# First expert group prepared inside the layers' last slots, and the softmax inverse placed behind a pass's third exponential

## The chip, the cores and the metric

One NeuronCore of one Trainium2 chip runs the whole program. The metric is the device time of one execution in microseconds (us), from the first to the last instruction and what lies around them. TensorE (PE), VectorE (DVE), ScalarE (ACT) and GpSimd (POOL) each run their own instruction list in order; SyncE (SP) issues all DMAs. They meet only at semaphores. An instruction that waits holds up everything behind it on its engine.

## The reference, cut to what matters

The input x is 32 sequences of 256 rows of 128 floats. Computed is `x1 = x + layers(layernorm(x))` and `out = x1 + experts(layernorm(x1))`.

```
h = layernorm(x)
for l in range(4):
    xn = ln(h) * w + b
    q, k, v = xn@Wq.T+bq, xn@Wk.T+bk, xn@Wv.T+bv            # 16 heads of width 8
    scores = (q.k + rel_shift((q+u).r)) * 8**-0.5, causal mask
    h = h + (softmax(scores) @ v) @ Wo.T + bo
    h = h + gelu(ln(h) @ W1.T + b1) @ W2.T + b2              # 512 wide
# experts: 16 of width 32 plus a shared one of width 256
s = sigmoid(xn @ router.T); sb = s + bias
keep the best 2 of 4 groups of experts, then the best 4 experts
w = s[chosen] / sum;  out = shared(xn) + sum_e w_e * down_e(silu(gate_e xn) * up_e xn)
```

## The kernel before, in words

**Layers.** `layers_program` treats (layer, sequence) as one index n from 0 to N-1 = 127 and is a software pipeline written out by hand: slot s of `SLOTS = range(-1, N + 6)` holds f1/f2/values of sequence s, the maxima scores of s-2, the attention scores of s-3 and s-4, the product with v of s-4, the output projection of s-5 and the feed-forward part of s-6. Each engine's block walks the same slots, with its own order inside a slot. Slots 0 to 127 are the body, 128 to 133 the tail in which ever fewer stages are live.

**The softmax division.** A column of ones in `v_pad` makes the product with v also give the denominators. ACT copies both out (`context_copy`, L850), SP sends the denominators to `ctx_den` and the numerators to `ctx_num` (L489, L492), ACT turns `ctx_den` into its inverse by a Ln and an Exp with scale -1 (`inverse`, L855 and L857), POOL multiplies (`normalize_context`, L1207), and PE's projection `b3` (L697) reads the product. `inverse(s - 5)` stands on ACT ahead of the three exponentials of rounds 1, 4 and 2 of sequence s-4 (`exp_round`, L818), and behind the copies `xn1T_out` (L826) and `xn2T_out` (L832). `split_first` (L841), gelu between two loads of activation tables (L902, L904), `context_copy` and the exponentials 5, 0, 3 follow.

**POOL's slot.** v_padded, xn2_split, normalize_context(s-5), turned(s-1) (L1185 to L1191), the next sequence's power (`power_in` for the first layer, L1131 to L1136; `power` for the others, L1140 and L1142), add_row twice (L1219), power of the second norm, xn1_split (L1167, L1169). In every 32nd slot `split_qkv` (L1150, L1152) stands at the slot's end.

**SP's slot.** The turned rows of q (L473, waits for `turned`), the maxima's rows (L481), the exchange (L453), the context (L489, L492), the q and k rows (L463, L465), and a load of weights or of x here and there. PE's `a_scores` round 5 (L656) waits for the maxima's rows to land.

**PE's slot.** Attention scores of rounds 1, 4, 2 among maxima scores, f2, values, up, `b3`, two products with v, maxima round 3, attention rounds 5, 0, 3, down (half), transposes, down (half).

**Experts.** `experts_program` runs after a barrier in a second block with 16 groups of 512 rows, again as slots, q from -1. In slot -1 group 0 is transposed, rounded in two parts (`exT_parts`), routed on DVE by a chain of small operations that wait for one another (L1589 to L1641), and the expert weights are split (L1557, L1559); POOL normalizes group 1 (`norm`, L1714). Already before the barrier, in slots N+3 and N+4 on DVE and N+4, N+5 on POOL, the residual and statistics of groups 0 and 1 and the norm of group 0 are made (L1033 to L1061, L1250, L1253).

The code of the four functions' places is printed here.

Of the kernel before, what the change touches and what calls it, by code (L numbers as in the profile page):

```python
# [28 lines left out]

# [16 lines left out]
N = LAYERS * B  # L46
# [37 lines left out]
EXP_SET, GELU_SET = "natural_log_exp_and_others", "gelu_and_others"  # L84
# [85 lines left out]
class Early:  # L170
# [17 lines left out]
    xn_ready: object  # L188


def early_parts(nc, ctx):
# [4 lines left out]
    def sem(name):  # L196
        return ctx.enter_context(nc.semaphore(name))

    return Early(
# [6 lines left out]
        ve_ready=sem("eve_ready"), rstd_ready=sem("erstd_ready"), xn_ready=sem("exn_ready"))  # L206


def layers_program(nc, a, h_all, ex):

    with ExitStack() as ctx:
# [9 lines left out]
        w_qkv = sb("w_qkv", [128, LAYERS, 3 * D])  # L221

# [34 lines left out]
        qstack = sb("qstack", [128, RING, PLACES, S], F32R)  # L257
        kstack = sb("kstack", [128, RING, PLACES, S], F32R)
# [262 lines left out]
        def _(pe):  # L521
# [213 lines left out]

            pe.wait_ge(first_landed, 32)

            for s in SLOTS:
# [37 lines left out]
                if live(s - 5):  # L776
                    b3(s - 5)
                if live(s - 4):
                    pv(s - 4, 1)
# [30 lines left out]
                if live(s - 6):  # L810
                    down(s - 6, 1)

        @block.scalar
        def _(act):
# [64 lines left out]
            for s in SLOTS:  # L879
# [4 lines left out]
                if live(s - 5):  # L884
                    inverse(s - 5)
# [4 lines left out]
                if live(s - 4):  # L890
                    exp_round(s - 4, 2)
                if s == 0:
# [22 lines left out]
        def _(dve):  # L915
# [154 lines left out]

            stats_1(0)
            for s in SLOTS:
# [48 lines left out]
                if s == N + 3:  # L1121
                    experts_stats()
                if s == N + 4:
                    experts_norm()
                    experts_stats_second()

        @block.gpsimd
        def _(pool):
# [109 lines left out]
            for s in SLOTS:  # L1238
# [4 lines left out]
                if live(s - 5):  # L1243
                    normalize_context(s - 5)
                if live(s - 1):
                    turned(s - 1)
                if s in (N + 4, N + 5):
                    g = s - N - 3
# [23 lines left out]
                if live(s + 4) and (s + 4) % B == 0 and s > 0:  # L1272
                    split_qkv(layer(s + 4))


def experts_program(nc, a, h_all, out, ex):
# [7 lines left out]
    with ExitStack() as ctx:  # L1284
# [14 lines left out]
        w_in_parts = sb("w_in_parts", [128, 2, 2 * GU], F32R)  # L1299
# [3 lines left out]
        xT = sb("exT", [128, 2, GT, 128])  # L1303
        xT_parts = sb("exT_parts", [128, 2, 2, GT, 128], F32R)
        score = sb("score", [128, GT, E])
        biased = sb("biased", [128, GT, E])
        larger = sb("larger", [128, GT * G, 2])
        smaller = sb("smaller", [128, GT * G, 2])
        tops = sb("tops", [128, 3, GT * G])
        gs = sb("gs", [128, GT, 14])  # L1310
        gtop = sb("gtop", [128, GT, 8])
# [474 lines left out]
```

## Time and profile before

| what | value |
|---|---|
| runs | 2225.02, 2231.17, 2236.08 us (median 2231.17) |
| profiled execution | 2229.07 us, span 2227.3 us |
| PE busy | 2152.8 us (97%) |
| PE weight loads busy | 1876.5 us (84%) |
| DVE, ACT, POOL busy | 1906.0 (86%), 1796.5 (81%), 1288.4 us (58%) |
| mean granted clock of PE | 0.988 |

The span is what lies between the first and the last instruction; the execution's own time is 1.77 us more. The barrier between the two blocks lies near 1956 us of the span. Busy means that the engine executed something other than waiting. Records of one engine may overlap by about 0.1 us.

### The profile page before, as it was taken

Reading aid. Unit: us, or ns where it says so; the run is one execution under the profiler, and the core shown is the slowest. Engines: PE = TensorE matmul, PEld = TensorE weight load, DVE = VectorE, ACT = ScalarE, POOL = GpSimd, SP = SyncE. Lnnn points to the kernel's source line nnn. Section 1 sums busy time; section 2 is a strip of 40 time slices with the busy share of each in tenths; the row PEclk is TensorE's granted clock in tenths of the full one; section 3 lists DMA queues with packets and bytes.
Section 4 is the critical chain, followed back from the end, with each engine's and each line's share of the span. In section 5 each row is a group of like instructions: output and inputs, shape, how many; then the busy total and the mean of one; then the engine's idle time right before and its main releaser. Section 6 shows DMA issues by size and latency. Waiting matters only on the chain. (4 is left out here: it accounts for less than half of the span.)

```text
span 2227.3 us, 80806 instructions
## 1 busy us (share of the span) xinstructions
PE 2152.8 (97%) x30224; PEld 1876.5 (84%) x30224; DVE 1906.0 (86%) x4659; ACT 1796.5 (81%) x2661; POOL 1288.4 (58%) x2277
## 2 busy tenths in 40 slices
PE   4899999999999999999999999999999999879999
PEld 3788888888888888888888888888888888768888
DVE  6789888888888888888888888888888888479996
ACT  2688888888888888888888888888888888845543
POOL 4555665566555555566555655565555555456774
PEclk8899999999999999999999999999999999979999
DMA  4444444444434444344443443344334444124443
GB/s 120 124 122 129 126 131 128 111 115 114 110 109 112 116 112 117 108 113 115 111 111 110 114 121 109 106 113 116 110 109 120 120 116 111 40 61 110 97 115 83
DMA packets 279984, 246.79 MB, mean 111 GB/s; under 512 B 38960, under 2 KB 270256, under 8 KB 279600
## 3 DMA queue, kind: packets, MB, share of 16 engines
q1 hardware_dynamic: 279600, 241.63, 40.0%
q8 instruction: 246, 4.03, 0.8%
q14 instruction: 138, 1.13, 0.2%
HBM read 31.24 MB, written 4.72 MB: 16 GB/s over the span
## 5 line engine op out<-in xcount | busy, mean ns | idle before, releaser
L1003 DVE TENSOR_REDUCE rowmax<-bank 128x4 f32<-128x1024 f32 (+1 forms) x768 | 916.3, 1218 | 149.5 <-PE bank L597 149.0
L818 ACT ACTIVATE probs<-bank 128x1024 f32<-128x1024 f32 x768 | 737.6, 1024 | 94.2 <-PE bank L656 82.9
L656 PE MATMUL bank<-qstack,kstack 64*128 64x128 f32 (+1 forms) x4096 | 423.2, 299 | 7.5 <-DMA qstack<-maxrows 7.3
L597 PE MATMUL bank<-kstack,qstack 62*128 62x256 f32 (+1 forms) x4096 | 417.7, 301 | 4.4 <-DMA qstack<-base_turned 4.4
L656 PEld LDWEIGHTS bank<-qstack,kstack 64*128 64x128 f32 x4096 | 315.0, 191 | 10.7 <-DMA qstack<-maxrows 10.1
L597 PEld LDWEIGHTS bank<-kstack,qstack 62*128 62x128 f32 x4096 | 317.3, 193 | 4.6 <-issue 4.6
L1167 POOL CAST xn1T_parts<-xn1T 128x256 fp32r<-128x256 f32 x128 | 50.7, 396 | 425.0 <-ACT xn1T L826 425.0
L731 PE MATMUL bank<-w,hidden 128*128 128x128 f32 x2048 | 284.1, 282 | 3.5 <-ACT hidden L866 2.8
L619 PE MATMUL bank<-maskT_half,pick_half 64*128 64x128 bf16 (+1 forms) x3072 | 268.7, 240 | 15.9 <-ACT probs L818 6.0
L676 PE MATMUL bank<-probs,v_pad 128*32 128x256 f32 x4096 | 271.0, 382 | 0.6 <-DVE v_tok L984 0.6
L559 PE MATMUL bank<-mask_half,pick_half 64*128 64x128 bf16 (+1 forms) x3072 | 269.5, 243 | 1.7 <-ACT xn1T L826 0.7
L731 PEld LDWEIGHTS bank<-w,hidden 128*128 128x128 f32 x2048 | 249.6, 192 | 21.7 <-issue 4.1
L1140 POOL TENSOR_SCALAR ve<-mv 128x2 f32<-128x2 f32 x224 | 49.6, 221 | 312.9 <-DVE mv L940 304.8
L841 ACT ACTIVATE base<-bank,b_cols 128x256 fp32r<-128x256 f32 x256 | 107.5, 470 | 130.6 <-PE bank L131 130.6
L866 ACT ACTIVATE hidden<-bank,b 128x256 f32<-128x256 f32 x512 | 200.6, 475 | 4.8 <-PE bank L131 3.3
L619 PEld LDWEIGHTS bank<-maskT_half,pick_half 64*128 64x128 bf16 x3072 | 116.6, 94 | 67.9 <-DVE rowmax L1003 24.9
L1142 POOL TENSOR_TENSOR rstd<-ve,expo 128x2 f32<-128x2 f32 x224 | 161.1, 719 | 18.7
L676 PEld LDWEIGHTS bank<-probs,v_pad 128*32 128x32 f32 x4096 | 117.3, 109 | 60.1 <-issue 0.8
L902 ACT ACT_TABLE_LOAD x128 | 164.2, 1283 | 2.3
L904 ACT ACT_TABLE_LOAD x128 | 164.2, 1283 | 2.3
L683 PEld LDWEIGHTS bank<-probs,v_pad 128*32 128x32 f32 x4096 | 122.4, 110 | 44.0
L683 PE MATMUL bank<-probs,v_pad 128*32 128x128 f32 x4096 | 158.7, 273 | 0.0
(147 smaller groups left out, 5008.9 us busy)
## 6 DMA issues: line engine op xcount, KB each, us to landing
qstack<-base SPq DMA_DIRECT2D x384, 128.0 KB, 2.6
kstack<-base SPq DMA_DIRECT2D x384, 128.0 KB, 2.6
qstack<-base_turned SPq DMA_DIRECT2D x384, 128.0 KB, 2.5
turn_x<-turn_c SPq DMA_DIRECT2D x512, 32.0 KB, 1.8
ctx_den<-ctxT_raw SPq DMA_DIRECT2D x256, 64.0 KB, 2.0
ctx_num<-ctxT_raw SPq DMA_DIRECT2D x256, 64.0 KB, 2.0
factors<-rows_kept SPq DMA_DIRECT2D x64, 256.0 KB, 4.8
h_all<-in_x SPq DMA_DIRECT2D x16, 256.0 KB, 3.2
```

The source lines that it names most:

```text
L559: pe.matmul(v[:, :, c:c + 64], pick_half[rows, half], mask_half[rows, half, 0:heads], start=(half == 0), stop=True, skip_group_check=True)
L597: last = pe.matmul(bank[:, b0 + b, i * wide:(i + 1) * wide], qstack[rows, r, p0 + i, t * 128:(t + 1) * 128], kstack[rows, r, p0 + i, 0:wid ...
L619: pe.matmul(v[:, :, c:c + 64], pick_half[rows, 2 + half], maskT_half[rows, half, 0:heads], start=(half == 0), stop=True, skip_group_check= ...
L656: last = pe.matmul(bank[:, b0 + b, i * wide:(i + 1) * wide], kstack[rows, r, p0 + i, kt * 128:(kt + 1) * 128], qstack[rows, r, p0 + i, q0: ...
L676: pe.matmul(bank[32 * c:32 * c + 32, PV_BANK, c0:c0 + S], v_pad[:, v, 0, 4 * half + c, w], x, start=(j == 0), stop=True, skip_group_check= ...
L683: last = pe.matmul(bank[32 * c:32 * c + 32, PV_BANK, c0 + 128:c0 + S], v_pad[:, v, 1, 4 * half + c, w], x, start=False, stop=True, skip_gr ...
L731: last = pe.matmul(bank[:, DOWN_BANK, t * 128:(t + 1) * 128], hidden[:, c, t * 128:(t + 1) * 128], w_2[:, layer(n), c], start=(c == 0), st ...
L818: act.activation(probs[:, k], bank[:, A_BANK[k]:A_BANK[k] + 2, :], ACT.Exp, scale=SCALE).then_inc(exp_done[k], 1)
L866: act.activation(hidden[:, c], bank[:, UP_BANK[c // 2], (c % 2) * S:(c % 2 + 1) * S], ACT.Gelu, bias=b_1[:, layer(n), c:c + 1]).then_inc(g ...
L902: act.preload_act_table_set(GELU_SET)
L904: act.preload_act_table_set(EXP_SET)
L1003: dve.tensor_reduce(rowmax[:, n % 2, t, :, p0:p0 + heads], bank[:, M_BANK[k]:M_BANK[k] + 2, :].rearrange("p b (h c) -> p b h c", h=heads), ...
```

## The change

There are two parts. In the first, the tiles and semaphores that group 0 of the experts needs move to the `Early` record that both programs share. `w_in_parts` now lies in the space of `qstack`, `exT_parts` in `kstack`, `exT` and the routing tiles in `w_qkv`, which are free late in the layers; so the new steps wait until their last readers are done. The routing functions become the class `Routing`, with the same operations. The statistics of group 0 and group 1 come two slots earlier; the experts' weights are split in slot N+2; group 0 is transposed in N+3 and routed in N+4. The experts' program then skips group 0's preparation and group 1's norm, which POOL does at the end of slot N+4.

In the second, `inverse` moves behind `exp_round(s - 4, 2)` on ACT, and `normalize_context` moves behind `turned` and the two power steps on POOL.

```
 PE, layers_program
+    def experts_turn():
+        pe.wait_ge(ex.landed, 16 * EX_DMAS); pe.wait_ge(ex.xn_ready, 1); pe.wait_ge(exp_done[0], N)
+        for t in range(GT):
+            last = pe.transpose(bank[:, X_TURN_BANK, t*128:(t+1)*128], ex.xn[:, t], ex.eye[:])
+    def experts_router():
+        pe.wait_ge(ex.xT_ready, 1)
+        for t in range(GT): last = pe.matmul(bank[:, X_TURN_BANK, t*E:(t+1)*E], xT[:, 0, t], ex.w_router[:], ...)
...
         b3(s - 5)
+        if s == N + 4: experts_router()
...
         down(s - 6, 1)
+        if s == N + 3: experts_turn()
 ACT
-                if live(s - 5):
-                    inverse(s - 5)
                 exp_round(s - 4, 1); exp_round(s - 4, 4); exp_round(s - 4, 2)
+                if live(s - 5):
+                    inverse(s - 5)
...
                     gelu(s - 6)
-                    act.preload_act_table_set(EXP_SET)
+                    if s < N + 4:
+                        act.preload_act_table_set(EXP_SET)
+                if s == N + 4:
+                    act.preload_act_table_set(SIGMOID_SET)
+                    act.wait_ge(ex.logits_done, 1)
+                    act.activation(ex.score..., bank[:, X_TURN_BANK, 0:GT * E], ACT.Sigmoid).then_inc(ex.score_ready, 1)
 DVE
+            def experts_weights():
+                dve.wait_ge(scoresT_done[A_LAST], N - RING + 2)
+                dve.tensor_copy(w_in_parts[:, 0], ex.w_in[:]); dve.tensor_tensor(w_in_parts[:, 1], ..., ALU.subtract)
+            def experts_turned():
+                dve.wait_ge(ex.xn_turned, 1)
+                dve.tensor_copy(xT[:, 0], bank[:, X_TURN_BANK, :]); dve.tensor_copy(xT_parts[:, 0, 0], xT[:, 0])
+                dve.tensor_tensor(xT_parts[:, 0, 1], xT[:, 0], xT_parts[:, 0, 0].bitcast(F32), ALU.subtract)
...
-                if s == N + 3:
+                if s == N + 1:
+                    dve.wait_ge(scoresT_done[A_LAST], N - RING + 2); dve.wait_ge(v_done, N)
+                    dve.wait_ge(weights_now, LAYERS)
+                    routing.fill()
                     experts_stats()
-                if s == N + 4:
+                if s == N + 2:
                     experts_norm()
                     experts_stats_second()
+                    experts_weights()
+                if s == N + 3:
+                    experts_turned()
+                if s == N + 4:
+                    routing.routing_groups_1(0); routing.routing_groups_2(0)
+                    routing.routing_experts(0); routing.weights_of_experts(0)
 POOL
-                if live(s - 5):
-                    normalize_context(s - 5)
                 if live(s - 1):
                     turned(s - 1)
-                if s in (N + 4, N + 5):
+                if s in (N + 2, N + 3):
                     ... (wait for mv_ready, ve, power: as before)
                 (power_in(s + 1) or power(..., s + 1))
+                if live(s - 5):
+                    normalize_context(s - 5)
                 add_row(s - 6, b_2, ...)
...
+                if s == N + 4:
+                    pool.wait_ge(ex.rstd_ready, 2); pool.wait_ge(ex.xn_turned, 1)
+                    for t in range(GT): last = pool.tensor_scalar(ex.xn[:, t], h_all[:, 2 + t // 2, t % 2], ...)
+                    last.then_inc(ex.xn_ready, 1)
 experts_program: every `if live(q + 1)` step of x_turn, router, xT_out, scores, low and routing gets
+ and q + 1 > 0
 norm(q + 2) is skipped for q + 2 = 1; the memsets of the routing tiles and the weights' split are gone;
-                load_table(2 * q, ACT.Sigmoid)
+                load_table(2 * q - 1, ACT.Sigmoid)
...
+            act.wait_ge(ex.route_filled, 2)
+            load_table(0, ACT.Silu)
```

## Rows read from the trace of the kernel before

**Rows 1.** Waits over the whole span: total us, times, longest us.

```profile
PEld bank L656 <- DMA qstack<-maxrows: 10.1, 14, 2.3
PEld bank L619 <- ACT probs L818: 9.1, 18, 1.4
```

**Rows 2.** Timeline of ACT, one first-layer slot: start, us, line; idle before, releaser.

```profile
263.81 2.86 ACT L818 ACTIVATE probs<-bank 128x1024 f32<-128x1024 f32 x3 [0.49 <-PE bank L656]
...
267.43 0.44 ACT L855 ACTIVATE ctx_den<-ctx_den 128x256 f32<-128x256 f32 x1
...
272.27 0.84 ACT L841 ACTIVATE base<-bank,b_cols 128x256 fp32r<-128x256 f32 x2 [0.89 <-PE bank L131]
```

**Rows 3.** The same timeline of ACT, the next slot's first exponentials.

```profile
278.43 2.86 ACT L818 ACTIVATE probs<-bank 128x1024 f32<-128x1024 f32 x3 [0.49 <-PE bank L656]
```

**Rows 4.** Timeline of POOL in the same first-layer slot.

```profile
269.98 0.73 POOL L1207 TENSOR_TENSOR ctx_num<-ctx_num,ctx_den 128x256 f32<-128x256 f32 x1
270.67 0.73 POOL L1185 TENSOR_TENSOR turn_x<-turn_s,turn_x 128x256 f32<-128x256 f32 x1
...
273.30 1.04 POOL L1136 TENSOR_TENSOR rstd<-ve,expo 128x4 f32<-128x4 f32 x1
```

**Rows 5.** Timeline of PE's weight loads, the projection of that slot.

```profile
273.83 0.53 PEld L697 LDWEIGHTS bank<-w_o,ctx_num 128*128 128x128 f32 x4
```

**Rows 6.** Timeline of POOL in a slot of the third layer.

```profile
1025.25 0.72 POOL L1142 TENSOR_TENSOR rstd<-ve,expo 128x2 f32<-128x2 f32 x1
```

**Rows 7.** Timeline of PE's weight loads, the projection of that slot.

```profile
1025.99 0.53 PEld L697 LDWEIGHTS bank<-w_o,ctx_num 128*128 128x128 f32 x4
```

**Rows 8.** Timeline of POOL, the slot after a split of the next layer's weights.

```profile
1372.12 0.40 POOL L1150 CAST w_now<-w_qkv 128x256 fp32r<-128x256 f32 x1
...
1378.01 0.72 POOL L1142 TENSOR_TENSOR rstd<-ve,expo 128x2 f32<-128x2 f32 x1
```

**Rows 9.** Timeline of PE's weight loads: that slot's projection.

```profile
1377.59 0.53 PEld L697 LDWEIGHTS bank<-w_o,ctx_num 128*128 128x128 f32 x4
```

**Rows 10.** Timeline of PE's weight loads: the wait for the maxima behind it.

```profile
1382.95 0.19 PEld L656 LDWEIGHTS bank<-qstack,kstack 64*128 64x128 f32 x2 [1.46 <-DMA qstack<-maxrows]
```

**Rows 11.** Timeline of ACT, a slot in which the denominators landed late.

```profile
1417.92 0.42 ACT L855 ACTIVATE ctx_den<-ctx_den 128x256 f32<-128x256 f32 x1 [1.22 <-DMA ctx_den<-ctxT_raw]
```

**Rows 12.** Timeline of PE's weight loads in the same slot.

```profile
1419.75 0.10 PEld L619 LDWEIGHTS bank<-maskT_half,pick_half 64*128 64x128 bf16 x2 [1.08 <-ACT probs L818]
```

**Rows 13.** Timeline of DVE in the tail and across the barrier.

```profile
1928.33 0.42 DVE L1069 TENSOR_TENSOR h_all<-bank,h_all 128x256 f32<-128x256 f32 x1 [3.90 <-PE bank L731]
...
1947.02 1.38 DVE L1061 TENSOR_SCALAR exn<-h_all,emv,erstd 128x128 f32<-128x128 f32 x4
...
1949.93 0.38 DVE L1055 BATCH_NORM_AGGREGATE emv<-estats 128x2 f32<-128x6 f32 x4
...
1957.52 1.76 DVE L1559 TENSOR_TENSOR w_in_parts<-w_in,w_in_parts 128x1536 fp32r<-128x1536 f32 x1
```

**Rows 14.** Timeline of PE's weight loads, the projection of sequence 126.

```profile
1932.49 0.53 PEld L697 LDWEIGHTS bank<-w_o,ctx_num 128*128 128x128 f32 x4
```

**Rows 15.** Timeline of POOL in the tail and across the barrier.

```profile
1943.83 0.71 POOL L1142 TENSOR_TENSOR rstd<-ve,expo 128x2 f32<-128x2 f32 x1
1946.34 0.40 POOL L1176 CAST xn2T_parts<-xn2T 128x256 fp32r<-128x256 f32 x1 [1.80 <-ACT xn2T L832]
...
1958.63 1.76 POOL L1701 TENSOR_TENSOR exT_parts<-exT,exT_parts 128x512 fp32r<-128x512 f32 x1 [6.18 <-ACT exT_parts L1511]
1960.39 3.17 POOL L1714 TENSOR_SCALAR exn<-h_all,emv,erstd 128x128 f32<-128x128 f32 x4
1966.08 1.28 POOL L1701 TENSOR_TENSOR exT_parts<-exT,exT_parts 128x512 fp32r<-128x512 f32 x1 [2.53 <-ACT exT_parts L1511]
```

**Rows 16.** Timeline of PE behind the barrier.

```profile
1956.53 0.63 PE L1423 MATMUL ebank<-eeye,exn 128*128 128x128 f32 x4 [1.18 <-PEq L211]
...
1963.61 1.12 PE L1423 MATMUL ebank<-eeye,exn 128*128 128x128 f32 x4 [4.11 <-POOL exn L1714]
```

More of the change, by code:

```diff
@@ L28 @@
 from dataclasses import dataclass
+import math
 import numpy as np
@@ L197, in sem, with part @@
         return ctx.enter_context(nc.semaphore(name))
+    qstack, kstack = (sb(name, [128, RING, PLACES, S], F32R) for name in ("qstack", "kstack"))
+    w_qkv = sb("w_qkv", [128, LAYERS, 3 * D])
+    w_flat, used = w_qkv[:].rearrange("p l c -> p (l c)"), [2 * GT * 128]
+    def part(*shape):
+        lo, n = used[0], math.prod(shape)
+        used[0] += n
+        flat = (w_flat[:, lo:lo + n] if used[0] <= LAYERS * 3 * D else sb(f"route_part{lo}", [128, n])[:])
+        return flat.rearrange("p (a b) -> p a b", a=shape[0]) if len(shape) == 2 else flat
     return Early(
@@ L734, in down @@
                     last.then_inc(down_done, 1)
+            def experts_turn():
+                pe.wait_ge(ex.landed, 16 * EX_DMAS)
+                pe.wait_ge(ex.xn_ready, 1)
+                pe.wait_ge(exp_done[0], N)
+                for t in range(GT):
+                    last = pe.transpose(bank[:, X_TURN_BANK, t * 128:(t + 1) * 128], ex.xn[:, t], ex.eye[:])
+                last.then_inc(ex.xn_turned, 1)
+            def experts_router():
+                xT = ex.xT()
+                pe.wait_ge(ex.xT_ready, 1)
+                for t in range(GT):
+                    last = pe.matmul(bank[:, X_TURN_BANK, t * E:(t + 1) * E], xT[:, 0, t], ex.w_router[:],
+                                     start=True, stop=True)
+                last.then_inc(ex.logits_done, 1)
             pe.wait_ge(first_landed, 32)
@@ L1471, in _ @@
             for q in SLOTS:
-                if live(q + 1):
+                if live(q + 1) and q + 1 > 0:
                     x_turn(q + 1)
@@ L1479, in _ @@
                     down(q - 1, 0)
-                if live(q + 1):
+                if live(q + 1) and q + 1 > 0:
                     router(q + 1)
@@ L1540, in _ @@
                     rows_out(q)
-                if live(q + 1):
+                if live(q + 1) and q + 1 > 0:
                     scores(q + 1)
@@ L1635, in weights_of_experts @@
[L1635 to L1642 removed]
+            routing = Routing(dve, ex, apart_dve)
@@ L1668, in _ @@
                     gating(q, 0)
-                if live(q + 1):
-                    routing_groups_1(q + 1)
+                if live(q + 1) and q + 1 > 0:
+                    routing.routing_groups_1(q + 1)
                 if live(q - 1):
@@ L1676, in _ @@
                     gating(q, 2)
-                if live(q + 1):
-                    routing_groups_2(q + 1)
+                if live(q + 1) and q + 1 > 0:
+                    routing.routing_groups_2(q + 1)
                 if live(q - 1):
@@ L1682, in _ @@
                     gating(q, 3)
-                if live(q + 1):
-                    routing_experts(q + 1)
+                if live(q + 1) and q + 1 > 0:
+                    routing.routing_experts(q + 1)
                 if live(q - 1):
@@ L1688, in _ @@
                     gating(q, 4)
-                if live(q + 1):
-                    weights_of_experts(q + 1)
+                if live(q + 1) and q + 1 > 0:
+                    routing.weights_of_experts(q + 1)
                 if live(q):
@@ L1724, in _ @@
             for q in SLOTS:
-                if live(q + 1):
+                if live(q + 1) and q + 1 > 0:
                     low(q + 1)
@@ L1728, in _ @@
                     power(q + 2)
-                if live(q + 2) and q + 2 > 0:
+                if live(q + 2) and q + 2 > 1:
                     norm(q + 2)
```

289 lines of the change are left out of this document (176 added, 113 removed).

## The prediction, on record before the changed kernel ran

> **What bounds the kernel now.** I read the page's busy shares first (PE 97%), then the waits over the whole span, then the timelines of ACT, POOL and PE's weight loads for a few slots side by side. The body of the layers repeats every 14.62 us: the exponentials of rounds 5, 0, 3 start at 263.81 and again at 278.43 [rows 2, 3], and most body slots have that length. In such a slot PE is never idle for more than a few tenths; it sets the length. The reader is to see two disturbances on top. When the maxima's rows land late, PE waits for them before attention round 5: 10.1 us in 14 waits [rows 1]. When the denominators land late, the inverse waits on ACT, the exponential of round 1 stands behind it, and PE waits for that exponential: 9.1 us in 18 waits [rows 1]; in one slot the inverse waited 1.22 us and PE 1.08 us [rows 11, 12].
>
> **The inverse behind the third exponential, ACT.** Nothing is added: Ln and Exp are 0.44 us each [rows 2]. Between the third exponential and `split_first` ACT idles 0.89 us for PE [rows 2], so the pair lands in that gap and `split_first` stays where it is, with no more than about 0.1 us at risk. If the gap is gone (a late pass), `split_first` and with it the cosines are late by what is missing. What it takes away: PE's waits for the first exponential. Of the 9.1 us I take away 7, since a part lies in the tail, where the exponentials themselves are late; bounds 0 and 9.
>
> **The product with the inverse, POOL.** This is where the change costs. POOL's list is dense from the split of xn1 to the second `add_row`, so moving the 0.73 us product behind `turned` and the power pulls these 0.69 us forward (270.67 - 269.98 [rows 4]) and ends the product where the power ended, plus 0.04. Nothing waits on the moved ones: their inputs, the exchange and the statistics, are microseconds old.
>
> - First layer. The power (four columns) ended at 273.30 + 1.04 = 274.34 [rows 4], so the product ends at 274.34 - 0.69 + 0.73 = 274.38. PE's projection began loading it at 273.83 [rows 5]. PE waits 0.55 us, with the handover 0.57. Behind that instruction on PE stand both products with v, maxima round 3, attention rounds 5, 0, 3; ACT's exponentials and so the next xn1 and POOL's next list hang on these, so the wait comes back every slot and nothing gives it back. 26 slots (projection live and next sequence still in layer 0) x 0.57 = +14.8 us. Bounds: 0 (PE has slack that records with modelled ends hide) and 26 x 0.65 = 17.
> - Other layers. The power ended at 1025.97 [rows 6]; the product ends at 1026.01, against a load at 1025.99 [rows 7]: 0.02, with the handover 0.04. 95 slots x 0.04 = +3.8 us. This is a tie within the resolution of the records; bounds -0.1 (no wait, 0 us) and 0.2 per slot (19 us). I take the value of the rows.
> - The slot after a split of the next layer's weights. There POOL starts 1.15 us late (1372.12 on [rows 8]). The old product was early enough to hide that; the new one ends at 1378.73 + 0.04 = 1378.77 against a load at 1377.59 [rows 9]: 1.18 us. Three such slots: +3.5 us; bounds 0 and 4.
> - The turned rows of q are ready 0.69 us earlier. SP's list waits for them, and the maxima's DMAs stand behind them, so these go out up to 0.69 us earlier as well; in the first layer PE comes 0.57 us later on top. That covers most of the 14 waits, and the one of 1.46 us behind the late POOL slot [rows 10], where PE itself now comes 1.2 us later. I take away 7 of the 10.1 us; bounds 0 and 10.
>
> Body: 14.8 + 3.8 + 3.5 - 7 - 7 = +8.1 us.
>
> **The tail.** In slots 127 to 130 the exponentials end close to the projection, so the inverse behind them makes the projection late by some tenths each; I take +1.0 in all (bounds 0 and four times 0.57, 2.3). In slot 131 POOL now makes group 1's power ahead of the product for sequence 126. It waits for group 1's statistics, and these start on DVE only after the residual add that ends at 1928.75 [rows 13]: norm of group 0 and the statistics last 1949.93 + 0.38 - 1947.02 = 3.3 us [rows 13], so they end at 1932.05. The add of 0.22 and the four-column power of 1.04 [rows 4] with their handovers give 1933.5, the product 1934.2, against a load at 1932.49 [rows 14]: +1.8 us, and the product with v, the last context and all that follows hang on it. In slot 132 the norm of group 1 (3.17 us [rows 15]) stands on POOL from the end of the power at 1944.54; the split of the last xn2 was at 1946.34 [rows 15] and can start at 1947.71: +1.4 us on the chain that ends the layers. The other additions are hidden: the filling and statistics of slot 129 in DVE's idle time before the next projection, group 0's transposes and router product in PE's idle time (they cost under 1.5 us), the split of xT where the statistics stood, the sigmoid's table load behind the gelu while ACT waits for the last xn2, and the routing chain between the last two residual adds. If that cover is gone, the routing would cost up to 7 us. Tail: +4.2 us; bounds 1 and 9.
>
> DVE's split of the expert weights (its second operation 1.76 us [rows 13]) now falls beside POOL's power and product. The rows show what such a meeting costs POOL: the rounding remainder took 1.76 us beside that operation and 1.28 alone [rows 15], so about 0.5. The Trainium skill's page SBUF — State Buffer (two separate sides) says the port pair that the two share is held for a whole instruction and the loser is blocked until its end. By the row the meeting costs 0.5, by the rule up to 1.76 us; the sum leaves it out as the overlap may not happen, and the range holds both.
>
> **The experts' start.** PE's first work is now the transposes of group 1, which it did at 1963.61 after POOL's norm, 4.11 us idle ahead of it; it can do them where group 0's stood, at 1956.53 [rows 16]: -7.1 us. Everything behind is as before. The x of group 2 is still only requested at the barrier, and the first gating stands behind its residual: +0.5 (bounds 0 and 2). That the transposes took 0.63 us at first and 1.12 us later [rows 16] tells that PE is slow in this stretch; how long it stays so may move by some us either way, which I put at nothing. Start: -6.6; bounds -8 and -2.
>
> **Sum.** 8.1 + 4.2 - 6.6 = +5.7 us on the profiled execution's own 2229.07: 2234.8 us. The runs' median is 2.1 us above that execution, so an offset of this size stays inside the band.
>
> **Rivals.**
> - The projection has slack. For it: the load at 273.83 need not be what PE needed at that moment, since loads run ahead of the matmuls. Against it: PE's list is in order and the load is followed within a tenth by its matmul. Then the body is 3.5 - 14 = -10.5, the whole -12.9: 2216 us.
> - Slower: the tie in layers 2 to 4 goes the wrong way. Place: POOL's list before the projection; price: 95 slots times what the chain is longer than the rows say, through the new neighbours of `turned` and power on DVE or a context that lands later. At 0.2 us per slot it is 19 instead of 3.8: +20.9, 2250 us. It decides from 0.11 per slot on (2241.5).
> - The late landings cost the same elsewhere. The transfers are as late as before, and PE waits for them at the projection or at round 5. For it: the SP list is itself full in slots with a load. Against: the inverse now has 3 us more. Both sevens return: +14, 2249 us.
> - Part one does nothing: the first products wait for something else (the factors' transfer, PE at low clock), and only the tail's costs stay: +6.6, 2241 us.
>
> **Chances and range.** Forecast 0.56; projection with slack 0.14; the tie lost 0.16; landings unchanged 0.08; part one without effect 0.06. About 0.5% (11 us) can be told from no change: below 2220 faster, above 2242 slower. So faster 0.14, same 0.62, slower 0.24. Range 2221 to 2249: it leaves out the first rival and the far end of the second. The forecast's own range is 2227 to 2241.
>
> **What would show it.** Right: POOL's product starts behind the power in every body slot; PE's projection load has an idle time of about 0.6 us with POOL as releaser in the first layer, next to none or under 0.1 in the others, about 1.2 in three slots; body slots of 15.2 and 14.65 us; the waits for probs and maxima down to a few us; the layers ending near 1956 + 12 us; group 1's transposes less than 1 us behind the barrier. Wrong: first-layer slots of 14.6 us, or later ones of 14.8 and more, or experts that last as long from the barrier as before.

## The result and the profile after

The changed kernel takes 2237.97 us (median of 14 runs, 2233.64 to 2241.83), the kernel before 2227.9 us on the same chips (14 runs). The ratio is 1.0042 [1.0031, 1.0054]: slower by 0.4%, inside what the forecast called the same, 3 us above its number. The change itself was larger than forecast: 10 us between the medians and 6.3 us between the two profiled executions, against a forecast of 5.7. The profiled execution has a span of 2233.6 us against 2227.3. Two terms of the sum were off by some 4 us each, in opposite directions. One run in what follows, of E6 with 2511.85 us, was in a slower state than all others and is left out of its ratio.

Where the 6.3 us between the two profiled executions lie is best seen by cutting both at the same instructions: the start of PE's first weight load for the output projection of a sequence, for PE's first work of the experts (before: group 0's transposes, after: group 1's, since group 0's are already done in the layers), and the end of the span. These are single executions, and runs of one kernel differ by some 5 us either way (2223.9 to 2236.1 for the kernel before), so a difference of 1 us in such a stretch is read only where rows show its cause.

| stretch, us | before | after | difference |
|---|---|---|---|
| start to the 2nd projection | 96.1 | 97.1 | +0.9 |
| layer 0 (25 slots) | 371.8 | 381.2 | +9.4 |
| layers 1 to 3 (96 slots) | 1412.9 | 1411.8 | -1.1 |
| last 5 projections | 60.6 | 68.3 | +7.7 |
| last projection to the experts' first PE work | 15.1 | 15.2 | +0.1 |
| from there to the end | 270.8 | 260.1 | -10.7 |

The waits over the whole span (engine, waiting tile and line, what it waited for: us in total, times, longest). L851 is the projection, L773 the first product with v, which reads the exponentials:

```profile
PEld bank L851 <- POOL ctx_num L1419: 26.3, 33, 3.9
PEld bank L773 <- ACT probs L992: 1.8, 2, 0.9
```

From the page's groups of instructions (busy, mean ns of one, idle time before them), attention's loads with the maxima:

```profile
L810 PEld LDWEIGHTS bank<-qstack,kstack 64*128 64x128 f32 x4096 | 315.6, 191 | 0.5 <-DMA qstack<-maxrows 0.4
```

So both kinds of late landing are nearly gone: 10.1 us for the maxima became 0.4, and 9.1 us for the exponentials 1.8 [rows 1]. A new wait of 26.3 us stands at the projection. One slot of layer 0 shows it; the timelines of ACT, POOL and PE's loads (start, duration, instruction, idle time before it and its releaser) answer to [rows 2 to 5]:

```profile
277.01 0.42 ACT L1031 ACTIVATE ctx_den<-ctx_den 128x256 f32<-128x256 f32 x1
277.55 0.84 ACT L1015 ACTIVATE base<-bank,b_cols 128x256 fp32r<-128x256 f32 x2
```
```profile
275.29 0.73 POOL L1397 TENSOR_TENSOR turn_x<-turn_s,turn_x 128x256 f32<-128x256 f32 x1
277.95 1.04 POOL L1348 TENSOR_TENSOR rstd<-ve,expo 128x4 f32<-128x4 f32 x1
278.96 0.73 POOL L1419 TENSOR_TENSOR ctx_num<-ctx_num,ctx_den 128x256 f32<-128x256 f32 x1
```
```profile
279.73 0.52 PEld L851 LDWEIGHTS bank<-w_o,ctx_num 128*128 128x128 f32 x4 [0.55 <-POOL ctx_num L1419]
```

The reader is to see that the inverse's second half (L1031) ends at 277.43, 1.5 us before the product (L1419) starts: ACT does not hold the product, POOL's own list does. The product ends at 279.69, and PE, idle 0.55 us, loads 0.04 us later. In a slot of the third layer the product directly follows a two-column power of 0.73 and there is no such wait; in the slot behind a split of the next layer's weights there is one of 1.12 us:

```profile
1021.24 0.73 POOL L1354 TENSOR_TENSOR rstd<-ve,expo 128x2 f32<-128x2 f32 x1
1021.94 0.73 POOL L1419 TENSOR_TENSOR ctx_num<-ctx_num,ctx_den 128x256 f32<-128x256 f32 x1
...
1389.93 0.72 POOL L1419 TENSOR_TENSOR ctx_num<-ctx_num,ctx_den 128x256 f32<-128x256 f32 x1
```
```profile
1390.71 0.52 PEld L851 LDWEIGHTS bank<-w_o,ctx_num 128*128 128x128 f32 x4 [1.12 <-POOL ctx_num L1419]
```

The slots last 15.22 us in layer 0 and 14.67 in the others, against 14.60 to 14.62 for an undisturbed slot before.

The tail is where more was lost than forecast. POOL, DVE and PE in slot 131 (answering to [rows 13, 14]):

```profile
1942.63 0.85 POOL L1460 TENSOR_SCALAR eve<-emv 128x4 f32<-128x4 f32 x1 [2.86 <-DVE emv L1235]
1943.56 2.51 POOL L1463 TENSOR_TENSOR erstd<-eve,expo 128x4 f32<-128x4 f32 x1
1946.05 0.72 POOL L1419 TENSOR_TENSOR ctx_num<-ctx_num,ctx_den 128x256 f32<-128x256 f32 x1
```
```profile
1942.46 0.93 DVE L1254 CAST qstack<-w_in 128x1536 fp32r<-128x1536 f32 x1
1943.42 1.76 DVE L1256 TENSOR_TENSOR qstack<-w_in,qstack 128x1536 fp32r<-128x1536 f32 x1
```
```profile
1946.82 1.22 PE L851 MATMUL bank<-w_o,ctx_num 128*128 128x128 f32 x4 [3.68 <-POOL ctx_num L1419]
```

One slot earlier, without DVE beside it, the same two instructions took 0.23 and 1.04 us:

```profile
1928.88 0.23 POOL L1460 TENSOR_SCALAR eve<-emv 128x4 f32<-128x4 f32 x1 [1.96 <-DVE emv L1220]
1929.20 1.04 POOL L1463 TENSOR_TENSOR erstd<-eve,expo 128x4 f32<-128x4 f32 x1
```

The first ends at 1943.48, 0.09 us behind the cast's end (1943.39), and the second at 1946.07, 0.9 behind the subtraction's end (1945.18). Alone they need 0.23 and 1.04 us, so each ended as if it had done all but 0.15 us of its work after DVE's instruction: 0.62 and 1.47 us were lost. The Trainium skill's page SBUF — State Buffer (SBUF: two separate sides) says that the port pair is held for a whole instruction and the loser blocked until its end. This trace agrees.

The 0.5 us that I took from [rows 15] was the price of a short meeting only. POOL's operation there started at 1958.63, when 0.65 us of DVE's subtraction was left (it ended at 1957.52 + 1.76 [rows 13]); it could lose no more than that, and lost 0.48.

The experts' start, PE behind the last residual add (DVE L1249, at 1972.62 + 0.42):

```profile
1973.53 0.63 PE L1618 MATMUL ebank<-eeye,exn 128*128 128x128 f32 x4 [1.01 <-PEq L367]
```

Group 1's transposes stand 0.49 us behind the end of the layers, where they stood 7.7 us behind it [rows 16]. Beyond these 7.2 us another 3.6 were gained. The windows (start:end and length, busy time of PE, PE's loads, DVE, ACT, POOL with their counts, granted clock as a share, DMA share, GB/s) of the first 40 us of experts, before and then after:

```profile
1956.50:1976.50 20.00, 14.43 (x48) 11.40 (x49) 15.21 (x75) 10.88 (x19) 10.61 (x12) 0.57 0.40 95
1976.50:1996.50 20.00, 17.01 (x81) 14.33 (x80) 15.24 (x68) 8.47 (x15) 11.95 (x13) 0.83 0.33 74
```
```profile
1973.50:1993.50 20.00, 14.89 (x70) 11.64 (x71) 15.20 (x66) 12.43 (x22) 11.89 (x12) 0.91 0.41 103
1993.50:2013.50 20.00, 20.00 (x112) 17.75 (x112) 14.86 (x69) 8.47 (x16) 12.01 (x13) 0.84 0.29 68
```

Before, the granted clock of the first 20 us was 0.57, near the lower of its two levels (1.2 GHz of 2.4 GHz, a share of 0.5); after, it was 0.91.

### The profile page after: what moved, and what is told of

It reads as the page before. It is cut to its first block and busy times, and to the rows that moved or that the text cites. A ratio compares the mean times of both kernels' runs of the same rounds, so it can differ in the third digit from the quotient of the medians.

```text
span 2233.6 us, 80802 instructions
## 1 busy us (share of the span) xinstructions
PE 2157.8 (97%) x30224; PEld 1880.1 (84%) x30224; DVE 1908.5 (85%) x4662; ACT 1790.9 (80%) x2656; POOL 1289.3 (58%) x2276
## 5 line engine op out<-in xcount | busy, mean ns | idle before, releaser
L773 PE MATMUL bank<-maskT_half,pick_half 64*128 64x128 bf16 (+1 forms) x3072 | 267.0, 240 | 9.8 <-DVE turn_c L1150 2.4
L773 PEld LDWEIGHTS bank<-maskT_half,pick_half 64*128 64x128 bf16 x3072 | 117.2, 94 | 62.0 <-DVE rowmax L1183 27.0
L133 PE MATMUL bank<-xn2T_parts,w_parts 128*128 128x256 f32 x512 | 156.0, 305 | 2.2 <-POOL xn2T_parts L1390 1.6
```

Of the source, the lines that this page charges most:

```text
L133: pe.matmul(out, w[0], x[0], start=True, stop=False)
L773: pe.matmul(v[:, :, c:c + 64], pick_half[rows, 2 + half], maskT_half[rows, half, 0:heads], start=(half == 0), stop=True, skip_group_check= ...
```

## The experiments

The change has two halves: the experts' first group inside the layers (first part), and the inverse behind the third exponential with its product on POOL behind the power (second part). Times in the table are medians; the ratio is against the kernel before on the same chip, with its 95% interval. It is formed from all runs of both kernels, so it need not be the quotient of the medians. E1 to E4 ran on one chip, E5 to E8 on a second, E9 and E10 on a third, where the kernel before took 2225.0, 2227.8 and 2226.4 us, so kernels are compared by their ratios.

| kernel | us | ratio |
|---|---|---|
| after | 2238.0 | 1.0042 [1.0031, 1.0054] |
| E1 first part only | 2225.1 | 0.9985 [0.9968, 1.0002] |
| E2 second part only | 2242.8 | 1.0073 [1.0051, 1.0094] |
| E3 product behind `turned` | 2212.9 | 0.9942 [0.9922, 0.9962] |
| E4 experts' power behind the product | 2230.5 | 1.0025 [1.0012, 1.0038] |
| E5 E3, norm of group 1 later | 2213.0 | 0.9934 [0.9919, 0.9949] |
| E6 E5, DVE's weight split one slot earlier | 2214.2 | 0.9944 [0.9923, 0.9966] |
| E7 E3, inverse back in its old place | 2216.5 | 0.9950 [0.9933, 0.9967] |
| E8 inverse moved, product not | 2557.4 | 1.1477 [1.1432, 1.1522] |
| E9 second part only, product behind `turned` | 2216.6 | 0.9942 [0.9919, 0.9965] |
| E10 only the product behind `turned` | 2220.0 | 0.9964 [0.9947, 0.9982] |

And the stretches of their profiled executions, cut as above (the last column runs from the experts' first PE work to the end of the span):

| us | start | layer 0 | layers 1-3 | last 5 | to experts | experts |
|---|---|---|---|---|---|---|
| before | 96.1 | 371.8 | 1412.9 | 60.6 | 15.1 | 270.8 |
| after | 97.1 | 381.2 | 1411.8 | 68.3 | 15.2 | 260.1 |
| E1 | 97.2 | 371.1 | 1417.4 | 63.8 | 17.0 | 259.0 |
| E2 | 98.8 | 381.1 | 1411.1 | 64.4 | 15.6 | 272.6 |
| E3 | 97.5 | 369.3 | 1405.8 | 63.7 | 15.2 | 260.8 |
| E4 | 96.7 | 382.1 | 1412.2 | 63.7 | 15.2 | 259.2 |
| E5 | 97.9 | 369.0 | 1406.8 | 63.7 | 13.6 | 260.9 |
| E6 | 96.5 | 368.0 | 1407.5 | 63.6 | 13.6 | 260.6 |
| E7 | 96.5 | 369.8 | 1412.1 | 62.1 | 16.9 | 262.2 |
| E8 | 94.8 | 438.8 | 1686.7 | 70.1 | 15.2 | 260.5 |
| E9 | 97.1 | 367.6 | 1404.9 | 62.5 | 12.7 | 267.1 |
| E10 | 95.9 | 370.9 | 1407.6 | 60.3 | 13.9 | 270.3 |

**E1, the first part alone.**

```diff
+                if live(s - 5):
+                    inverse(s - 5)
                 if live(s - 4):
                     exp_round(s - 4, 1)
...
-                if live(s - 5):
-                    inverse(s - 5)
...
+                if live(s - 5):
+                    normalize_context(s - 5)
                 if live(s - 1):
                     turned(s - 1)
...
-                if live(s - 5):
-                    normalize_context(s - 5)
```

> Only the first part (group 0 of the experts prepared in the layers' last slots); inverse and product stand where they stood before. Theory (the body's loss comes from the product's new place on POOL, the experts' start gains about 11 us by the traces): body slots as in the kernel before (14.60 us and the old disturbances), tail longer by 1.4 us (norm of group 1 ahead of the last xn2 split) and 1.5 us (DVE's weight split ahead of a residual add), experts 10.9 shorter: about 8 us faster than before. Rival (the tail's additions cost what the start gains): within 3 us of before. Rival (the losses of the body come from the memory moves of the first part): slower than before by 5 us or more.

It measured 0.9985, -3 us, not to be told from nothing: the expected 8 us missed, and the rival in which the tail takes what the start gives came closest (within 3 us). The late landings are back, as large as before:

```profile
PEld bank L773 <- ACT probs L992: 12.0, 23, 1.4
PEld bank L810 <- DMA qstack<-maxrows: 11.1, 12, 2.4
```

The experts gained as in the changed kernel (270.8 to 259.0), but 5 us went in ahead of them: 3.2 in the last five projections and 1.9 behind these, and layers 1 to 3 took 4.5 more with their late landings. In this execution the first part alone moves a good part of its gain from the end of the kernel into the tail.

**E2, the second part alone**: the kernel before with the same two moves, in the other direction of E1's diff.

> Only the second part (inverse behind the third exponential, product behind the power). Theory: PE waits 0.54 us at the projection in each of 25 first-layer slots, 1.1 to 1.7 in three slots, 0.07 per slot in the others; maxima and exponential waits gone; body +9, tail +1.5, so about 10.5 us slower than before. If the parts added, first part -8 and second +10.5 would give +2.5 for both; both together showed +6 in the trace, and theory says that the difference is POOL's long power behind DVE in the tail, which only the pair has. Rival (the second part is neutral and the loss is an effect of both): within 3 us of before.

It measured 1.0073, some 16 us slower where 10.5 were expected. Its layers are those of the changed kernel to within 1 us in both stretches (its start is 1.7 us longer), and its waits are nearly the same:

```profile
PEld bank L697 <- POOL ctx_num L1207: 24.8, 33, 3.3
PEld bank L619 <- ACT probs L818: 1.8, 2, 0.9
PEld bank L656 <- DMA qstack<-maxrows: 1.4, 2, 1.2
```

So the new wait and the end of the two old ones belong to the second part alone. The experts, whose code is that of before, took 272.6 against 270.8 us, with a granted clock in their first two windows of 20 us of 0.66 and 0.74 against 0.57 and 0.83.

The halves add up within their intervals: 0.9985 x 1.0073 = 1.0058, against 1.0042 together.

**E3, the product one place earlier.** If the wait at the projection is POOL's order and not ACT's inverse, the product directly behind `turned` (ahead of the power) keeps what the second part gains and loses its price.

```diff
                 if live(s - 1):
                     turned(s - 1)
+                if live(s - 5):
+                    normalize_context(s - 5)
...
-                if live(s - 5):
-                    normalize_context(s - 5)
                 if live(s - 6):
                     add_row(s - 6, b_2, ...)
```

> Both parts, but POOL's product stands right behind the turned rows, ahead of every power step. Theory: the product then ends at about 1.0 us ahead of the projection in all slots but the three behind a weight split, so the 0.54 us waits (25 slots), the 0.07 (95 slots) and most of the three long ones go, while the turned rows keep their 0.69 us and the maxima do not return; the 3.9 us wait in the tail goes too: 14 + 6.5 + 2.5 + 3.5 less, 26 us faster than the changed kernel, 2211 to 2213 us, 0.7% faster than before. Rival (the late landings only hide behind the wait at the projection and come back when it goes): no more than 14 us faster than the changed kernel, 2224 us. Rival (the power behind the product becomes the late one: first norm's rstd on DVE): slots of 14.9 us or more in the first layer.

It measured 2212.9 us, 0.6% faster than the kernel before. By the ratios that is 22 us faster than the changed kernel (the 25 us between the medians come from two chips), where 26 were expected and the rival gave no more than 14. The wait at the projection fell from 26.3 to 3.9 us:

```profile
PEld bank L810 <- DMA qstack<-maxrows: 5.0, 8, 1.6
PEld bank L851 <- POOL ctx_num L1419: 3.9, 5, 1.6
...
POOL ctx_num L1419 <- ACT ctx_den L1031: 39.8, 123, 3.4
```

The last line is a wait that appears on POOL: 0.3 us per slot for the inverse. It costs next to nothing: the median slot is 14.63 us in layer 0 and 14.62 in the others, as an undisturbed one before. An engine's wait is a price only if its consumer is late, as the changed kernel shows from the other side: there POOL waits 5.0 us in all for the inverse, and the kernel is slower.

**E4, the experts' power behind the product**, in slots 130 and 131, all else as in the changed kernel. It takes two things off the product's path at once: the power itself, and the power's meeting with DVE on the port pair.

```diff
-                if s in (N + 2, N + 3):
-                    ... # wait for the statistics, add, power of group s - N - 1
                 if live(s + 1) and 0 < s + 1 < B:
                     power_in(s + 1)
...
                 if live(s - 5):
                     normalize_context(s - 5)
+                if s in (N + 2, N + 3):
+                    ...
```

> Both parts; on POOL only the experts' power steps of the two tail slots stand behind the product in place of ahead of it; the body is unchanged. Theory: the body stays at 15.22 and 14.67 us, the waits at the projections of sequences 125 and 126 fall from 0.7 and 3.9 us to 0.7 and about 0.6, about 3.5 us faster than the changed kernel. The four-column power itself still takes about 2.5 us beside DVE's weight split, off the path. Rival (the chain through the inverse on ACT is as long): under 1 us.

The last five projections went from 68.3 to 63.7 us, and the ratio from 1.0042 to 1.0025: 4 us, as expected (3.5), though the two intervals overlap. POOL (first fence) and DVE (second):

```profile
1943.85 1.08 POOL L1419 TENSOR_TENSOR ctx_num<-ctx_num,ctx_den 128x256 f32<-128x256 f32 x1 [3.12 <-ACT ctx_den L1031]
1944.91 1.74 POOL L1466 TENSOR_SCALAR eve<-emv 128x4 f32<-128x4 f32 x1
1946.72 1.04 POOL L1469 TENSOR_TENSOR erstd<-eve,expo 128x4 f32<-128x4 f32 x1
```
```profile
1943.42 0.93 DVE L1254 CAST qstack<-w_in 128x1536 fp32r<-128x1536 f32 x1
1944.39 2.16 DVE L1256 TENSOR_TENSOR qstack<-w_in,qstack 128x1536 fp32r<-128x1536 f32 x1
```

The power is back at 1.04 us, where the expectation kept it at 2.5. The meeting has not gone but moved: now the product met DVE's cast and took 1.08 us instead of 0.73, DVE's subtraction started beside the product and took 2.16 instead of 1.76, and the small operation ahead of the power took 1.74 instead of 0.23, off the product's path. E4 does not tell the price of the power's place from that of the meeting.

**E5, E3 with the norm of group 1 one slot later**, behind the split of the last xn2 and `add_row`, so that the split no longer stands behind 3.1 us of norm. **E6** moves DVE's split of the expert weights (`experts_weights`) from slot N+2 to N+1 on top.

```diff
+                if s == N + 5:
+                    ... # norm of group 1
...
-                if s == N + 4:
-                    ...
```

And E6 on top of it, on DVE:

```diff
                 if s == N + 1:
                     ...
+                    experts_weights()
                 if s == N + 2:
                     ...
-                    experts_weights()
```

> The kernel with the product right behind the turned rows, and POOL's norm of group 1 one slot later, behind the last xn2 split and row add. Theory: in the changed kernel the norm (3.14 us) ends and the last split starts at once, 0.9 us after its input; with the norm behind it the last split waits only for ACT's xn2T, so the layers end 0.9 to 1.4 us earlier and the experts start as before (the norm ends about 3 us ahead of the barrier): 1 us faster than the kernel with the product behind the turned rows, 2212 us. Rival (the norm then ends behind the barrier): no gain or a loss of up to 2 us in the experts' stage.

> As the kernel with the norm behind the split, and DVE's weight split in slot N+1 in place of N+2. Theory (DVE and POOL meet: DVE's split ahead of the residual add of sequence 126 delays it, and POOL's power beside it takes 2.5 us instead of 1.04): in N+1 DVE has 3.0 us idle ahead of the next residual add, so the split is hidden there, the four-column power of N+2 moves back to 1.04 us if no other DVE operation with two inputs from memory runs beside it, and that of N+1 becomes the long one; another 1 us faster. Rival (POOL's product for sequence 125 meets the split and is late by up to 2 us): no gain or 1 us slower.

E5's stretch from the last projection to the experts fell from 15.2 to 13.6 us. Of these 1.6 us, 1.3 lie where the norm stood: PE loads the last split xn2 6.23 us behind the last projection, against 7.52 in E3 and 6.24 in the kernel before. In the total that is too little to tell E5 (0.9934) from E3 (0.9942), though E5 has the lowest ratio of the study.

E6 brought nothing, and its rival says why: the product for sequence 125 now met DVE's subtraction, and PE waited 1.78 us for it where it had waited 0.72 in E5. POOL, DVE and PE's loads:

```profile
1912.14 1.78 POOL L1419 TENSOR_TENSOR ctx_num<-ctx_num,ctx_den 128x256 f32<-128x256 f32 x1 [3.31 <-ACT ctx_den L1031]
```
```profile
1911.58 1.76 DVE L1256 TENSOR_TENSOR qstack<-w_in,qstack 128x1536 fp32r<-128x1536 f32 x1
```
```profile
1913.97 0.52 PEld L851 LDWEIGHTS bank<-w_o,ctx_num 128*128 128x128 f32 x4 [1.78 <-POOL ctx_num L1419]
```

The later intervals were shorter in turn, and the last five projections took 63.6 us against 63.7.

**E7, E3 with the inverse back ahead of the exponentials.**

> As the kernel with the product behind the turned rows, but the inverse on ACT back ahead of the three exponentials. It separates what the move on ACT brings from what the move on POOL brings. Theory: the waits of PE for the exponential (5.9 us in the body's trace before, 8.8 in that with the first part alone) come back, the maxima's stay at a few us, since they hang on POOL's turned rows: body 5 to 8 us longer than with the product behind the turned rows, 2219 us. Rival (late transfers are one cause, and the exponential's waits were bought by the maxima's): the body differs by under 2 us. Rival (ACT's move brings nothing since the exponentials wait for PE anyway): under 1 us.

It measured 2216.5 us, 2 us more than E3 by the ratios (0.9950 against 0.9942), with intervals that overlap. In its profiled execution, which is 5 us above its median, layers 1 to 3 took 6.3 us more than in E3. The landings are late again for the exponentials:

```profile
PEld bank L773 <- ACT probs L992: 10.2, 19, 1.1
PEld bank L810 <- DMA qstack<-maxrows: 4.2, 3, 2.2
```

**E8, the inverse moved and the product not**: what the second part would be without its POOL half.

```diff
+                if live(s - 5):
+                    normalize_context(s - 5)
                 if live(s - 1):
                     turned(s - 1)
...
-                if live(s - 5):
-                    normalize_context(s - 5)
```

> Both parts, inverse behind the third exponential, but POOL's product where it stood before, ahead of the turned rows. Theory: POOL then waits for the inverse about 2.2 us in every slot, the turned rows, SP's issue and the maxima's rows land 2.2 us later, and PE waits at attention round 5 for about 2 us in nearly all slots: body slots of 16 to 17 us, 2227 + 120 * 1.7 = about 2430 us. Rival (the turned rows have room): under 2260 us.

It measured 2557 us in two runs, 14.8% slower, and worse than either theory (2430 us, and under 2260). POOL now waits for the inverse in every slot, `turned` stands behind it, and PE stands behind the maxima of the turned rows:

```profile
POOL ctx_num L1419 <- ACT ctx_den L1031: 288.4, 127, 3.4
...
PEld bank L810 <- DMA qstack<-maxrows: 247.7, 124, 3.4
```

That is 2 us per slot. The profile pages of the changed kernel (first) and of E8 show a second cost:

```profile
PE 2157.8 (97%) x30224; PEld 1880.1 (84%) x30224; DVE 1908.5 (85%) x4662; ACT 1790.9 (80%) x2656; POOL 1289.3 (58%) x2276
```
```profile
PE 2284.6 (89%) x30224; PEld 1992.5 (78%) x30224; DVE 2001.5 (78%) x4662; ACT 1806.3 (70%) x2656; POOL 1292.3 (50%) x2276
```

The span grew by 332.5 us (2566.1 against 2233.6). Of these PE was idle for 206 more and busy for 127 more, with the same number of matmuls, and its granted clock was 0.940 over the span against 0.989. So a slot takes 17.6 us on average and not the 16 to 17 of the theory, which had counted the waits alone. PE's timeline in a slot shows the same group of four matmuls at 0.48 us ahead of the wait and 0.78 behind it, and eight matmuls of the MLP at 1.77 and then 1.06:

```profile
1011.50 0.48 PE L751 MATMUL bank<-kstack,qstack 62*128 62x256 f32 x4
...
1013.99 0.33 PE L810 MATMUL bank<-qstack,kstack 64*128 64x128 f32 x2 [1.88 <-DMA qstack<-maxrows]
...
1014.88 0.78 PE L751 MATMUL bank<-kstack,qstack 62*128 62x256 f32 x4
...
1016.78 1.77 PE L885 MATMUL bank<-w,hidden 128*128 128x128 f32 x8
...
1019.04 1.06 PE L885 MATMUL bank<-w,hidden 128*128 128x128 f32 x8
```

**E9 and E10**, on the kernel before, without the first part: E9 moves the inverse and puts the product behind `turned`; E10 does only the latter.

```diff
-                if live(s - 5):
-                    normalize_context(s - 5)
                 if live(s - 1):
                     turned(s - 1)
+                if live(s - 5):
+                    normalize_context(s - 5)
```

> The kernel before with the inverse behind the third exponential and the product right behind the turned rows; nothing of the first part. Theory: body as with both parts and the product behind the turned rows, 10 us shorter than before by traces (disturbances gone), tail longer by 1 us, experts' stage unchanged: 9 us faster than before, ratio 0.996. With the second part as it was changed (1.0073) this says that one place on POOL is worth 25 us. Rival (the gain of 12 to 14 us with both parts came mostly from the experts' start): under 4 us faster.

> The kernel before with only POOL's product behind the turned rows; the inverse stays ahead of the exponentials. Theory: the maxima's waits of PE (7.8 us in the body) fall to 2 to 4, those for the exponential (5.9 us) stay: 4 to 5 us faster than before, ratio 0.998, and about 5 us slower than with the inverse moved as well. Rival (the order of transfers shifts late ones from one wait to the other): within 1 us of before.

E9 has the ratio of E3, 0.9942, with the experts left as they were; 0.996 was expected. E10, one exchange of two neighbours on POOL, gives 0.9964, where 0.998 was expected. Their waits, E9 and then E10:

```profile
PEld bank L656 <- DMA qstack<-maxrows: 4.4, 6, 2.2
PEld bank L697 <- POOL ctx_num L1207: 4.2, 6, 1.6
```
```profile
PEld bank L619 <- ACT probs L818: 7.0, 12, 0.9
PEld bank L656 <- DMA qstack<-maxrows: 4.1, 6, 1.2
```

E2 and E9 differ in the product's place alone, behind the power or ahead of it: 1.0073 against 0.9942, 29 us.

## Why the forecast held, step by step

**The projection's wait in layer 0** was right in mechanism and size: 0.53 to 0.56 us in nearly each of the slots, forecast 0.57, slots of 15.22 us against 15.2. Layer 0 grew by 9.4 us and not 14.8, because its disturbances went at the same time, which the sum has in other terms: the 25 slots took 6.3 us more than 25 undisturbed ones before, and 0.7 more after. E3 takes it away and layer 0 falls to 369.3. The rival in which the projection has slack is out.

**Layers 1 to 3** were right: 14.67 us per slot (forecast 14.65), so the tie went as the rows said, and the three slots behind a split waited 1.71 (this one lies in the stretch of layer 0), 1.14 and 1.12 us (forecast 1.18 each). Layers 1 to 3 came out 1.1 us shorter in sum, since before they took 10 us more than 96 undisturbed slots, and after 3.5.

**The two sevens** (landings) were right in mechanism and a little low: the maxima's waits fell by 9.7 us, the exponentials' by 7.3, 17.0 in all for 14. Body in all: +0.9 + 9.4 - 1.1 = +9.2, forecast +8.1. E10 shows that both kinds of wait shrink in part (10.1 to 4.1 and 9.1 to 7.0) by the exchange on POOL alone, so pulling `turned` forward is what reaches the maxima; E7 and E10 against E3 and E9 show that the exponentials' waits need the inverse moved. What the inverse is worth in time is 0.1 to 0.2% by both pairs, with intervals that overlap: likely, not shown.

**The tail** was mis-sized: +7.7 us in the last five projections and +0.1 behind them, forecast +4.2 in all. The step that failed is "+1.8 us" for POOL's power ahead of the product in slot 131: PE waited 3.7. I had the meeting with DVE's split of the expert weights at hand and left it out of the sum; it cost 2.1 us on POOL (0.62 + 1.47). E4, which undoes the order, gives back 4.5: 2.8 in the interval that holds this wait and 1.7 in the next one. PE's granted clock was at its lower level for 6.8 us from 1945.4 on, that is from within the 3.7 us without work, and 5.4 us of them lie in this next interval. In E4 there is no such stretch in it:

```profile
1945.40:1952.20 6.80, 5.38 (x52) 3.29 (x56) 1.76 (x7) 1.57 (x2) 3.67 (x6) 0.50 0.00 1
```

So the wait seems to have cost more than its own length; no run shows that alone. The small terms in slots 127 to 130 were low as well: the inverse behind the exponentials costs 2.2 us in the last five projections (E9 less E10) or 1.6 (E3 less E7), forecast 1.0. The norm of group 1 on the chain was right up to the last split of xn2: forecast 1.4 us, 1.3 measured, given back in E5. Yet the stretch as a whole grew by 0.1 only, since what lies behind that split took 7.7 us and not 8.9. PE's clock was at its lower level for 6.8 us of it before and for 3.5 after, which fits; that this is the cause was not shown.

**The start of the experts** was mis-sized the other way: -10.9 us from the last residual add, forecast -6.6. The transposes' move was right (7.2 us, forecast 7.1). The step that failed is the one that put PE's slow clock "at nothing". From the experts' first PE work on, the kernels that still prepare group 0 there took 270.8, 272.6, 267.1 and 270.3 us (before, E2, E9, E10), and the eight that don't 259.0 to 262.2. Within the first set the one with the better clock is the shortest; the first 40 us of E9:

```profile
1944.80:1964.80 20.00, 13.76 (x62) 10.71 (x63) 18.02 (x99) 12.19 (x21) 10.77 (x12) 0.83 0.38 95
1964.80:1984.80 20.00, 17.65 (x90) 14.85 (x88) 15.21 (x64) 8.15 (x15) 16.07 (x15) 0.83 0.33 74
```

Counting what the clock withholds as the missing share of these windows, it is (0.43 + 0.17) x 20 = 12.0 us before, 6.8 in E9 and (0.09 + 0.16) x 20 = 5.0 after. E9 is 7.0 us longer than after, about the move of the transposes; before is 10.7 longer, and withholds 7 us more. E10 and E2 withhold 12.0 as before does, and last 270.3 and 272.6. E7 withholds 9.2 and is 1.4 us longer than E3, which differs from it in the inverse's place alone and withholds 5 as after does. But kernels with the same clock as after here lie between 259.0 and 260.9 us, so a difference of 2 us says little. That the clock makes up the 3.6 us beyond the move, or most of them, is likely and not shown: it is a reading of single executions, no experiment was made on the clock alone, and what sets it at this point stays open.

The two errors, +4 and -4, cancelled by luck, so the total was closer than the terms deserved. There was luck in the base as well: the forecast stands on the profiled execution's 2229.07 us, 1.2 above the median of the kernel before, so that 10 us between the medians still landed 3 us from the number.

**The first part** does almost nothing: 0.9985 alone, and 0.9942 with or without it once the product stands right (E3, E9). It saves 6 to 8 us of experts (E9 to E3 267.1 to 260.8, E10 to E7 270.3 to 262.2) and pays back about 1.5 us in the last five projections (1.2 and 1.8 in the same pairs), 2.5 to 3.0 behind these, and the 4.5 of the meeting where the power stands ahead of the product. These are pairs of single executions, and the small remainder is below what these runs can tell.

## What to carry to other kernels

A moved instruction is priced at both ends of its engine's list: what comes forward where it stood, and behind what it now ends; then its end is held against its consumer's start, slot by slot, the slots with extra work on their own. Here one place in POOL's order was worth 22 to 29 us (E3 against the changed kernel, E9 against E2), more than everything else that the change did, so the neighbouring places of a moved instruction are worth a run each. And where one move needs another (the inverse moved alone costs 14.8%, the product moved alone gains 0.4%), the pair is best tried in the mended order before either is judged.

## What was not expected of the hardware

- A small operation of POOL that meets a long one of DVE loses what is left of DVE's instruction, less some 0.15 us, whatever its own length. Six meetings in these traces:

| POOL's operation, its time alone | beside DVE's | DVE's time left at its start | lost |
|---|---|---|---|
| TENSOR_SCALAR 128x4, 0.23 us (E4) | subtraction | 1.64 | 1.51 |
| power 128x4, 1.04 (after) | subtraction | 1.62 | 1.47 |
| product 128x256, 0.73 (E6) | subtraction | 1.20 | 1.05 |
| TENSOR_SCALAR 128x4, 0.23 (after) | cast | 0.76 | 0.62 |
| remainder 128x512, 1.28 (before, [rows 15]) | subtraction | 0.65 | 0.48 |
| product 128x256, 0.73 (E4) | cast | 0.50 | 0.35 |

- The other way round, DVE's subtraction in E4 started with 0.54 us of POOL's product left and took 2.16 us instead of 1.76.
- In E8 a wait of about 2 us on PE in every slot of 17.6 us went with a granted clock of 0.94 over the whole span, and with single groups of matmuls at 1.6 times their time (0.78 against 0.48 us). PE's idle time grew by 206 us and its busy time by 127, so the waits cost three fifths more than their own length.
